# Opening statistics ahead of constants on VectorE, and filler products in front of more kinds of TensorE work, in longer planned holes alone

## The reference, cut to what matters

```python
x = x + attention(layernorm(x), w_qkv, w_out)                 # 16 heads of 16, causal
x = x + cp_mumoe(layernorm(x), proj, C1, Win1, Wout1, ...)    # entmax gate, gelu, rank 128
x = x + latent_attention(layernorm(x), Wq_down, ..., Wc)      # rotary on half of each head, causal
x = x + squared_relu_ffn(layernorm(x)) + routed experts       # routed part only where prob truncates to 1
```

## Time and profile before

| | |
|---|---|
| median of 3 runs | 3037.79 us (3033.26 to 3039.56) |
| profiled execution, its own time | 3033.58 us |
| its span, first to last instruction | 3031.9 us |
| mean granted TensorE clock | 0.978 |
| PE busy | 2849.9 us, 94% |
| DVE / ACT / POOL busy | 68% / 65% / 40% |
| filler products on PE | 178 |

### The profile page before, as it was taken

The page is one execution under the profiler, slowest core; times in us unless marked ns, Lnnn a source line. Parts: engine busy times, 40 slices in busy tenths (PEclk is TensorE's granted clock), DMA queues, the critical chain, the costliest instruction groups (busy, mean ns, idle before and its releaser), DMA issues.

```text
span 3031.9 us, 55430 instructions
## 1 busy us (share of the span) xinstructions
PE 2849.9 (94%) x17865; PEld 1365.7 (45%) x17865; DVE 2074.2 (68%) x5654; ACT 1957.8 (65%) x3868; POOL 1213.8 (40%) x2540
## 2 busy tenths in 40 slices
PE   5898999999999999999999999999999999999987
PEld 3334443445434454445534454344543445444533
DVE  3683677666877678685786758776687767867473
ACT  3465666776657766676667766577666776667544
POOL 2324461445415362263623545143531537225411
PEclk8899999999999999999999999999999999999989
DMA  5612452334423353234522435133442335333140
GB/s 170 147 27 67 97 112 48 86 99 110 98 56 87 93 125 88 55 104 90 143 56 56 128 86 123 38 88 96 114 108 42 96 96 131 71 63 80 45 105 16
DMA packets 241197, 268.27 MB, mean 88 GB/s; under 512 B 19568, under 2 KB 208912, under 8 KB 240912
## 3 DMA queue, kind: packets, MB, share of 16 engines
q1 hardware_dynamic: 240912, 264.66, 36.8%
HBM read 162.35 MB, written 100.66 MB: 87 GB/s over the span
## 4 chain that ended last, share of the span: by engine, by line
PE 70%; DVE 13%; ACT 8%; issue 3%; DMA 3%; SPq 2%; POOL 1%; DVEq 0%; ACTq 0%; POOLq 0%
PE ps L1159 16%; PE ps L1141 13%; PE ps L1116 12%; PE ps L1096 6%; PE ps L1088 6%; DVE mx L1726 5%; ACT probs L1455 4%; PE ps L1237 4%; PE ps L1232 3%; DMA stk_k<-k 3%; DVE ps L1723 2%; PE ps L1224 2%; PE ps L1076 2%; ACT xn L1404 1%; PE ps L1121 1%
## 5 line engine op out<-in xcount | busy, mean ns | idle before, releaser
L1455 ACT ACTIVATE probs<-ps 128x512 f32<-128x512 f32 (+1 forms) x2432 | 1229.4, 587 | 355.7 <-PE ps L1141 349.2
L1726 DVE TENSOR_REDUCE mx<-ps 128x1 f32<-128x512 f32 (+2 forms) x1408 | 886.9, 682 | 240.5 <-PE ps L1116 177.7
L1630 POOL TENSOR_SCALAR_AFFINE_SELECT probs<-probs 128x128 f32<-128x128 f32 (+2 forms) x1408 | 476.1, 345 | 1277.0 <-ACT probs L1455 1247.7
L1723 DVE CUSTOM_DVE_ANT_0 ps<-ps,mask_b 128x512 f32<-128x512 f32 (+1 forms) x1024 | 614.1, 649 | 316.0 <-PE ps L1116 313.5
L1116 PE MATMUL ps<-stk_k,stk_q 112*128 112x512 bf16 (+3 forms) x3072 | 771.5, 333 | 34.5 <-DVE mx L1726 11.7
L1141 PE MATMUL ps<-stk_q,stk_k 115*128 115x512 bf16 (+3 forms) x3072 | 751.4, 328 | 16.7 <-ACT probs L1455 9.2
L1159 PE MATMUL ps<-probs,vaug 128*17 128x512 f32 (+3 forms) x6144 | 580.6, 490 | 15.4 <-POOL probs L1630 10.2
L1141 PEld LDWEIGHTS ps<-stk_q,stk_k 115*128 115x128 bf16 x3072 | 270.6, 97 | 436.4 <-issue 220.1
L1116 PEld LDWEIGHTS ps<-stk_k,stk_q 112*128 112x128 bf16 x3072 | 276.2, 98 | 399.3 <-issue 251.3
L1159 PEld LDWEIGHTS ps<-probs,vaug 128*17 128x17 f32 x6144 | 137.0, 96 | 324.6 <-issue 203.5
L1088 PE MATMUL ps<-turned,wqkv 128*128 128x512 f32 x512 | 263.7, 610 | 6.8 <-ACT turned L1391 3.7
(11 more groups left out here) (153 smaller groups left out, 3005.4 us busy)
## 6 DMA issues: line engine op xcount, KB each, us to landing
k<-parts SPq DMA_DIRECT2D x128, 384.0 KB, 3.4
stk_q<-q SPq DMA_DIRECT2D x256, 192.0 KB, 4.1
stk_k<-k SPq DMA_DIRECT2D x128, 384.0 KB, 6.3
q<-parts SPq DMA_DIRECT2D x64, 384.0 KB, 3.0
stk_k<-k SPq DMA_DIRECT2D x128, 192.0 KB, 4.2
x<-in_L_attn_x SPq DMA_DIRECT2D x16, 512.0 KB, 5.0
k<-parts SPq DMA_DIRECT2D x64, 128.0 KB, 3.4
stk_q<-q SPq DMA_DIRECT2D x128, 64.0 KB, 6.4
```

Source lines behind the costliest of these rows:

```text
L1455: act.activation(probs[:, step % PBUF, h:h + k, cols], src, ACT.Exp, scale=SCALE)\
L1630: pool.affine_select(out=diag, in_=diag, compare_op=ALU.is_ge, fill=0.0, base=0, pattern=[[0, k]] * (k > 1) + [[1, P]], channel_multiplier ...
L1723: dve.tensor_tensor_reduce(tile, tile, mask_b[:, BANK - width:BANK], 1.0, LOWEST, ALU.add, ALU.max, most)\
L1726: dve.tensor_reduce(most, tile.rearrange("q (k w) -> q k w", k=k), AX.X, ALU.max)\
```

## The change

It has two parts, and the list `ORDER` and the assignment of banks are the same in both kernels.

First, DVE takes the statistics of (0, 0) and (0, 1) and then writes the long constants. Two waits for `ready0` are added: ACT's also ahead of the first `vaug` copy of the half (0, 1), and SP's ahead of the first load of a stack.

Second, the filler products. A planned gap now counts if it is over 0.7 us (`FILL_FROM`), and it counts ahead of every kind of item; `keep_going` is called also ahead of scores (`s`), of all `st` tiles, of the transposes of the maxima (`mt`) and of the narrow products (`lg`, `rt`). The number is still the gap over 0.25 us. From `FILL` of both kernels: 36 products go (two ahead of `st` at 16 places, one at four places), 182 are added, 324 stand in the new kernel. The added ones: 20 ahead of `mt` of unit 0 and 9 behind it; 7 ahead of `mt` of unit 6 and of units 35, 51, 67, 83, 99, 115; 16 ahead of `mt` 8 and 6 ahead of `mt` 23; 4 in the midst of the scores of units 33, 49, 65, 81, 97, 113 and 119; 7 in those of unit 20; 23 in those of units 8 and 9; 12 in those of unit 124; 3 ahead of an `st` of unit 7; 9 ahead of `lg` and `rt`.

```diff
@@ program_order
+        made = len(plan.order)
         elif what == "chain":
-            item = plan.chains[args[0]][0][0][0]
-            if item[0] in ("xt", "yt", "at") and gap > FILL_TIME:
-                FILL[item] = int(gap / FILL_TIME)
             given[args[0]] += plan.give(args[0])
         elif what == "st":
...
-            if j == 0 and h == 0 and gap > FILL_TIME:
-                FILL["st", u, j, h] = int(gap / FILL_TIME)
...
         if what != "wait":
+            item = plan.order[made]
+            if gap > FILL_FROM and item[0] in ("xt", "yt", "at", "st", "mt", "s", "nm", "lg", "rt"):
+                FILL[item] = int(gap / FILL_TIME)
             gap = 0.0
...
-FILL_TIME = 0.25
+FILL_TIME, FILL_FROM = 0.25, 0.7
@@ SP, load_stack
+                if u == 0:
+                    sp.wait_ge(ready0, 2)
@@ PE, score
+                n, (out, done) = packed(width), claim(("s", u, i, h, p))
+                keep_going(("s", u, i, h, p), out)
                 pe.wait_ge(stk_loaded[slot], 16 * STACK_DMAS * (u // NBUF + 1))
-                n, (out, done) = packed(width), claim(("s", u, i, h, p))
@@ PE, max_rows
                 pt, done = claim(("mt", u))
+                keep_going(("mt", u), pt)
@@ PE, scores_t
                 out, done = claim(("st", u, j, h))
+                keep_going(("st", u, j, h), out)
                 if j == 0 and h == 0:
-                    keep_going(("st", u, j, h), out)
                     pe.wait_ge(m_loaded, 16 * (MT["mt", u] + 1))
@@ PE, narrow_product
+                pt, done = claim(key)
+                keep_going(key, pt)
                 need_xT(n, b, c)
-                pt, done = claim(key)
@@ ACT, copy_v
-                if (b, l, c, tp) == (0, 0, 0, 0):
+                if (b, l, tp) == (0, 0, 0):
                     act.wait_ge(ready0, 2)
@@ DVE
-            dve.memset(vaug[:], 1.0)
-            for i in range(NBUF):
-                dve.memset(stk_k[ROWS_A:P, i, :, :], -1.0)
-            dve.memset(o_bank, 0.0)
-            dve.wait_ge(pool_chain, 8)
-            dve.drain().then_inc(ready0, 1)
+            def fill_constants():
...
...
                     statistics(0, c, x[:, x_slot(b, c)], range(TPC))
+                    if (b, c) == (0, 1):
+                        fill_constants()
```

More of the change, by code:

```diff
@@ L1898, in _ @@
             dve.memset(going[:, :, 0:1], 0.0)
-            dve.memset(vaug[:], 1.0)
-            for i in range(NBUF):
-                dve.memset(stk_k[ROWS_A:P, i, :, :], -1.0)
-            dve.memset(o_bank, 0.0)
-            dve.wait_ge(pool_chain, 8)
-            dve.drain().then_inc(ready0, 1)
+            def fill_constants():
+                dve.memset(vaug[:], 1.0)
+                for i in range(NBUF):
+                    dve.memset(stk_k[ROWS_A:P, i, :, :], -1.0)
+                dve.memset(o_bank, 0.0)
+                dve.wait_ge(pool_chain, 8)
+                dve.drain().then_inc(ready0, 1)
             for item in ORDER:
```

## The result

The changed kernel takes 2998.63 us, median of four runs (2997.53 to 3001.2). The kernel before took 3037.1 us beside it (3033.26 to 3039.56). The ratio is 0.9875, with a 95% interval of 0.9864 to 0.9887: it is faster by 38.5 us. The forecast was 3014.0 us with a range from 3001 to 3029, so the sign was right and the gain some 60% larger than foretold; the time lies 2.4 us under the range. Two more sessions gave 2999.6 against 3034.3 and 2997.87 against 3035.0, gains of 34.7 and 37.1 us.

What follows compares the result with a forecast made beforehand. PE was taken to bound the kernel, busy 2849.9 of 3031.9 us. Terms -13.1 - 5.0 + 6.0 - 11.7 - 2.5 = -26.3 us, shortened to -24; from 3037.8 that gave 3014.0 us, range 3001 to 3029.

Steps and rivals of the forecast that it cites:

- The start: Statistics ahead of the long constants: PE's first transposes come near 14.0 instead of 27.11 us, gaining 13.1 us.
- start is eaten: Rival, chance 0.06: the early chain meets something unseen, such as weight loads; at most 5 us kept, about 3026 us.
- POOL blocked by constants: Rival, chance 0.03: POOL's `rstd` waits until DVE has written `vaug`, 4.5 us off the gain, 3018.5 us.
- Pairs taken out: 36 filler products removed, mostly two ahead of an `st` tile: saves 5.0 us, bounds 0 and 7.8.
- Products put in: 182 added filler products, 39.2 us of PE work, mostly absorbed in waits: costs 6.0 us.
- the place near the end: 3 and 5 added products around 2891.09 us, with nothing there to absorb them: costs 2.5 us.
- The six places in scores: 4 products in scores, as at unit 49, mostly absorbed by a later wait for `y`: about 0.1 us left each time.
- The clock in the eight places: Waits around `nm`, `mt`, `at` before the first feed-forward part: filling them wins half of 23.5 us lost at 0.50, 11.7.
- The shortening to -24: Whole kernel: sum cut from -26.3 to -24 us because a clock gain frees PE to wait for DVE next.
- The clock behind the first maxima: PE work from 89.82 us on, about 6 us, should run in 3: gains 2.5 us, bounds 0 to 4.4.
- products cost what the clock gives: Rival, chance 0.20: clock falls come anyway, fewer products are absorbed, only the earlier statistics pay: 3024.7, up to 3029 us.
- products behind the waits: Rival, chance 0.05: where the hole is a wait for a bank, products run after it; if all paid, 3056.1 us.

Runs made afterwards that it cites:

- part 1 alone: The changed kernel with the statistics ahead of the long constants but the old 178 filler products: 3020.68 us, ratio 0.9952 to the kernel before.

## Why the prediction was right and wrong, by its steps

**The start: right.** Forecast 13.1 us; 13.0 at the first transposes, 13.2 in the median of part 1 alone. That all of it stays was less exact: the first maxima's transposes, forecast near 72.4, came at 72.04 to 73.72 in three profiles. The rival "start is eaten" didn't come. The constants end at 28.49, as forecast, and ACT's first `vaug` copy, forecast for 30.7, came at 31.43: the wait has more to spare than I thought.

**POOL blocked by constants: no.** `rstd` took 1.02 us as before, though `vaug` was being written from 11.31 on, and `shift` took its 0.20 us at 11.72, wholly beside it. The clause of the Trainium skill (SBUF — State Buffer, Who interferes with whom) that an instruction with at most one SBUF input outside the 2-port modes doesn't contend agrees with this trace.

**Pairs taken out: wrong, 5.0 us forecast, 0 to 1 measured.** The step "nearer to the upper one, since no idle time stands behind the pair" failed. It looked one item ahead; less than 3 us later PE goes by DVE's maxima anyway, and the pairs only shift that wait.

**Products put in: 6.0 us forecast, about half of that seen.** No run gives the whole term, only parts of it. The 2.5 us for the place near the end were not seen: without the 16 products of units 119 and 124 the trace loses 1.9 us behind unit 116 rather than gaining. The six places in scores cost near 0.5 us each instead of 0.1, 2.9 us in all. The 7 ahead of each `mt` cost 0.12 us at unit 51, as the text had it. The 39 around units 8 and 9 neither cost nor bring much: from unit 7 to unit 9 the kernels with them lose 0.2 to 0.4 us against before and those without them, with the clock at 0.50 there, 0.4 to 0.5.

**The clock in the eight places: the step that failed.** The mechanism was right, the size was not: I took half of 23.5 us, 11.7, although I wrote that the rows spoke for no fall, because they were few and every place might fall otherwise once the start moved. It didn't: part 1 alone has all eight. All eight vanished. They are worth 16.6 us between the two profiles, 17.3 us when taken out of the changed kernel, 23.2 us when put alone into the kernel before. All three include what the products themselves cost. In the trace of the last, the shift grows by 16.3 us at the places, measured as for the changed kernel, and by 5.8 between them, from unit 21 to unit 114. Part 1 alone drifts by 3.4 us in the same stretches, without any product added, so part of it is how one execution differs from another; the rest I leave open. Since pairs and products nearly cancel, in the forecast (5.0 against 6.0) as in the runs (0 to 1 against about 3), this one term makes the miss: part 2 was put at 10.9 us after the shortening and brought 22.4, and the term was put at 11.7 and brought up to 23.2. PE's busy time, forecast to fall, rose by 4.0 us: half of the 47.0 us at the eight places is 23.5, and 146 more products at 0.2155 us are 31.5.

**The shortening to -24: wrong.** The reason, that a gain in clock frees PE to wait for DVE, is a real effect (at 277 us it eats the whole gain), but at unit 51, one of the eight places, the first `st` tile comes 1.8 us sooner (8.78 us behind `nm` instead of 10.57), and the gain stays.

**The clock behind the first maxima: right.** Forecast 2.5; 2.8 lost when the 9 products go. In the changed kernel's trace the lead grows by 3.1 us from the first maxima's transposes (11.8) to unit 3 (14.9), in that of part 1 alone by 0.6.

**The rival "products cost what the clock gives": no.** Its argument that falls come elsewhere instead finds one small case: after the start moved, the fall at 208 us grew from 3.4 us to some 10 in part 1 alone, which loses 2.5 us there (from -14.0 to -11.5 at unit 7). The rival "products behind the waits" has its mechanism in the sets of 4 products in scores, where half is paid, but not its size.

## What to carry to other kernels

Where a trace shows TensorE's clock at half speed again and again behind the same piece of program, add up the short waits just ahead of it and fill one of the longest with dummy products; here 56 of them, 12 us of PE work, brought 23 us. Which of two adjoining waits they stood in made no difference in the traces; twice as many cost 7 us. Judge a clock fall by who sets the pace in it: ten microseconds at 0.50 cost nothing here where VectorE was busy throughout, while 7 us of it cost 2 to 3 us where TensorE set the pace. An item that comes earlier is no gain until the next wait behind it has been read too.

## What the runs showed of the hardware

The clock fell to 0.50 (1.2 GHz) with no single wait over 1 us ahead of it: waits of 0.81, 0.21, 0.92, 0.84 and 0.30 us among work were enough, at every one of six places, in the kernel before (0.81, 0.22, 0.84, 0.84 and 0.29) and in two more. The Trainium skill (TensorE: Matmul & The Clock Gate, Why this matters for your kernels) warns of a long idle gap between bursts; these falls had no such gap. With nearly the same idle time the falls came at some of six alike places and not at others (1 of 6, 2 of 6). Where such falls are left, the time of an execution goes with its granted clock. Of the six executions without the 56 products the fastest, 3007.91 us, had 0.987 and the slowest, 3019.43, had 0.983; 0.004 of 3012 us is 24 us more at 0.50, which is worth 12 us if TensorE sets the pace throughout, an estimate, and 11.5 were measured. Eleven executions of the kernel before run from 3030.04 us at 0.979 to 3041.17 at 0.975. So one profile shows how many falls one execution had, and not how many the kernel has.
